# Two-layer gated cross-attention and routed experts on one core: counts read per expert, a second row buffer, and an earlier weight conversion

## The reference, cut to what matters

```python
# layer 0: 8 experts, the best 4 for each token, hidden size 1024
routing_weights = softmax(x @ router_w)
topk_weights, topk_indices = top_k(routing_weights, 4)
topk_weights = topk_weights / sum(topk_weights)
h = gelu(einsum('bsd,edh->bseh', x, up_w))
out = sum over the chosen e of topk_weight * (h_e @ down_w[e])
# layer 1: 8 experts, the best 2, biases b1 and b2, exact gelu
x = x + tanh(g_ffn[layer]) * out
```

## Time and profile before

| | us |
|---|---|
| median of 3 runs | 1605.39 (1602.2 to 1613.03) |
| the profiled execution | 1604.2 |
| its span, first to last instruction | 1602.3 |
| experts of layer 0 in it, from the first branch | 500 to 962 |
| experts of layer 1 in it, lists and end included | 1289 to 1602.3 |

### The profile page before, as it was taken

The page is one execution under the profiler, slowest core; times in us unless marked ns, Lnnn a source line. Parts: engine busy times, 40 slices in busy tenths (PEclk is TensorE's granted clock), DMA queues, the critical chain, the costliest instruction groups (busy, mean ns, idle before and its releaser), DMA issues. The chain is left out here.

```text
span 1602.3 us, 25436 instructions
## 1 busy us (share of the span) xinstructions
PE 1392.9 (87%) x9908; PEld 1288.8 (80%) x9908; DVE 834.8 (52%) x1654; ACT 713.1 (45%) x1375; POOL 552.5 (34%) x389
## 2 busy tenths in 40 slices
PE   5899989899867999999989995999889678987996
PEld 5776858768647899899889995988888668987996
DVE  3655656655664446446435223556666865455421
ACT  3354444444343454444444443454343425443553
POOL 1200001001025466566565441122120266566543
PEclk8899999999987999999999997998989769998998
DMA  3302031110115343443442223021202165444222
GB/s 128 120 24 67 27 95 43 52 61 27 66 51 156 94 86 81 116 106 92 105 104 47 47 42 100 24 88 41 72 30 80 54 193 119 102 106 109 48 42 35
DMA packets 72147, 123.30 MB, mean 77 GB/s; under 512 B 7440, under 2 KB 53152, under 8 KB 71968
## 3 DMA queue, kind: packets, MB, share of 16 engines
q1 hardware_dynamic: 46816, 81.92, 15.6%
q0 software_dynamic: 25152, 39.01, 13.4%
HBM read 96.12 MB, written 24.79 MB: 75 GB/s over the span
## 5 line engine op out<-in xcount | busy, mean ns | idle before, releaser
L2324 DVE TENSOR_TENSOR m_hidden_lo<-m_act_out,m_hidden_hi 128x512 fp32r<-128x512 f32 x224 | 162.6, 727 | 393.9 <-ACT m_hidden_hi L2267 368.5
L395 PE MATMUL banks<-m_down_hi,m_hidden_hi 128*128 128x256 f32 x896 | 267.9, 299 | 17.5 <-DVE m_hidden_lo L2324 11.3
L395 PE MATMUL banks<-m_down_hi,m_hidden_lo 128*128 128x256 f32 x896 | 263.7, 294 | 1.5 <-issue 1.5
L395 PE MATMUL banks<-m_down_lo,m_hidden_hi 128*128 128x256 f32 x896 | 263.9, 295 | 0.3 <-issue 0.3
L395 PEld LDWEIGHTS banks<-m_down_hi,m_hidden_hi 128*128 128x128 f32 x896 | 181.6, 203 | 22.2 <-issue 20.4
L395 PE MATMUL banks<-m_xt_hi,m_up_hi 128*128 128x256 f32 x640 | 186.6, 291 | 6.4 <-issue 6.4
L395 PE MATMUL banks<-m_xt_lo,m_up_hi 128*128 128x256 f32 x640 | 183.2, 286 | 0.0
L395 PE MATMUL banks<-m_xt_hi,m_up_lo 128*128 128x256 f32 x640 | 183.1, 286 | 0.0
L395 PEld LDWEIGHTS banks<-m_down_hi,m_hidden_lo 128*128 128x128 f32 x896 | 181.1, 202 | 1.7 <-issue 1.7
L395 PEld LDWEIGHTS banks<-m_down_lo,m_hidden_hi 128*128 128x128 f32 x896 | 181.5, 203 | 0.6 <-issue 0.6
L2401 POOL DMA_INDIRECT m_other_block<-rows,list_i x116 | 120.8, 1042 | 148.5 <-DVE list_i L1453 100.6
(11 more groups left out here) (367 smaller groups left out, 3555.0 us busy)
## 6 DMA issues: line engine op xcount, KB each, us to landing
stage<-in_down SPq DMA_DIRECT2D x22, 512.0 KB
stage<-in_ctx_cols SPq DMA_DIRECT2D x26, 402.0 KB
stage<-in_ctx_rows SPq DMA_DIRECT2D x20, 512.0 KB
stage<-in_up SPq DMA_DIRECT2D x20, 512.0 KB
m_stage<-in_up SPq DMA_DIRECT2D x11, 512.0 KB
m_stage<-in_down SPq DMA_DIRECT2D x10, 512.0 KB
rows<-xn SPq DMA_DIRECT2D x8, 528.0 KB, 3.7
stage<-in_ctx_picked SPq DMA_DIRECT2D x8, 512.0 KB
```

The costliest lines, as they stand in the source:

```text
L395: mm = q.e.matmul(dst, a, b, start=first and n == 0, stop=last and n == 2, skip_group_check=True)
L2324: q.e.tensor_tensor(lo, m.act[(n * HP + h) % ACTS], f32(hi), ALU.subtract).then_inc(*hidden_lo.mark((layer, n, h)))
```

## The change

Three things change.

1. Each engine loads the count of an expert when it reaches that expert's branches, after block (e, 0), instead of all eight at the head (`count_of`, called by `blocks`). The counting matmul and the copy of its result come ahead of the four steps that write the lists.
2. Blocks with j > 1 have two row buffers, by j even or odd. The second lies in the memory of the tables `onehot`, which are not needed while experts are computed. Block (e, j) gathers (e, j+3) now, and block (e, 0) gathers both (e, 2) and (e, 3), at its head. POOL's block (e, 0) is a function of its own, `gpsimd_opening`.
3. DVE converts quarters 2 and 3 in one go ahead of the low part of pair 0.

```diff
@@ counts
-        def counts(q, layer):
+        def count_of(q, layer, e):
+
             q.wait_ge(*route_dve.of("count", layer))
-            return [q.e.snap(q.e.value_load(counts_i[0:1, e:e + 1], min_val=0, max_val=BATCH * TOK)) for e in range(E)]
+            return q.e.snap(q.e.value_load(counts_i[0:1, e:e + 1], min_val=0, max_val=BATCH * TOK))
...
-        def blocks(q, layer, held, own, e, j, block):
+        def blocks(q, layer, own, e, block):
+            further(q, layer, count_of(q, layer, e), own, e, 1, block)
+
+        def further(q, layer, held, own, e, j, block):
...
@@ row buffers
-                m.other = sb(n + "other_block", [P, BT, ROW], F32, st)[:, :, :]
+                m.other = [sb(n + "other_block", [P, BT, ROW], F32, st)[:, :, :], rows_there]
...
-            return m.other if j > 1 or (e, j) == (0, 0) else m.second if j else m.first
+            return m.other[j % 2] if j > 1 or (e, j) == (0, 0) else m.second if j else m.first
...
-            return numbered(e, j - 1) if j > 2 else numbered(e - 1, NB - 1) if j == 2 else numbered(e - 1, j)
+            return numbered(e, j - 2) if j > 3 else numbered(e - 1, NB - 4 + j) if j > 1 else numbered(e - 1, j)
@@ vector_block
+            if more:
+                q.wait_ge(*down_done.of(layer, n - 1, HP - 1))
+                convert(q, "d", [quarter(layer, e + 1, x) for x in range(KD, 4)])
             for h in range(HP):
                 vector_low(q, layer, e, j, h)
...
-                if more and h >= 2:
-                    q.wait_ge(*down_done.of(layer, n - 1, HP - 1))
-                    convert(q, "d", [quarter(layer, e + 1, KD + h - 2)])
@@ gpsimd_gather
-            if j == 2 and (layer or e):
-
-                q.e.wait_ge(other_in.sem, q.e.snap(others_begun[0]))
+            if j in (2, 3) and (layer or e):
+
+                q.e.wait_ge(there.sem, q.e.snap(others_begun[j % 2]))
@@ gpsimd_block
-            n, more = numbered(e, j), j == 0 and e + 1 < E
-            gpsimd_added(q, layer, n - 2)
-            if 0 < j < NB - 1:
-                gpsimd_there(q, layer, e, j + 1)
-            if (e, j) == (1, 0):
+            n = numbered(e, j)
+            if j != 1:
+                gpsimd_added(q, layer, n - 2)
+            if j == 0:
+                gpsimd_opening(q, layer, e)
+                return
+            if 1 < j < NB - 2:
+                gpsimd_there(q, layer, e, j + 2)
+            gpsimd_add(q, layer, e, j)
+            if j + 3 < NB:
+                gpsimd_gather(q, layer, e, j + 3)
+
+        def gpsimd_opening(q, layer, e):
+
+            n, following = numbered(e, 0), [quarter(layer, e + 1, x) for x in range(4)] if e + 1 < E else []
+            gpsimd_gather(q, layer, e, 2)
+            gpsimd_gather(q, layer, e, 3)
+            if e == 1:
                 gpsimd_gather(q, layer, 2, 0)
-            if more:
-                convert(q, "p", [quarter(layer, e + 1, x) for x in range(KD)])
+            convert(q, "p", following[0:KD])
             if n:
-                gpsimd_add(q, layer, e, j)
-            if j + 2 < NB:
-                gpsimd_gather(q, layer, e, j + 2)
-            if more:
-                convert(q, "p", [quarter(layer, e + 1, x) for x in range(KD, 4)])
+                gpsimd_add(q, layer, e, 0)
+            gpsimd_there(q, layer, e, 2)
+            gpsimd_there(q, layer, e, 3)
+            convert(q, "p", following[KD:4])
+            if following:
                 gpsimd_gather(q, layer, e + 1, 1)
-                if e and e + 2 < E:
-                    gpsimd_gather(q, layer, e + 2, 0)
-            if j == 0:
-                convert(q, "p", ahead(layer, e - 1))
+            gpsimd_added(q, layer, n - 1)
+            if e and e + 2 < E:
+                gpsimd_gather(q, layer, e + 2, 0)
+            convert(q, "p", ahead(layer, e - 1))
```

More of the change, by code:

```diff
@@ L1517, in tensor_count, with vector_count, vector_finish_lists @@
                 *route_pe.mark(use))
-        def vector_finish_lists(q, layer):
+        def vector_count(q, layer):
             use = ("count", layer)
             q.wait_ge(*route_pe.of(*use))
+            q.wait_ge(*added.of(layer - 1, "all"))
+            q.e.tensor_copy(counts_i[:, :], gen.of(use)[0:1, 0:E]).then_inc(*route_dve.mark(use))
+        def vector_finish_lists(q, layer):
             q.wait_ge(*route_dve.last())
-            q.e.tensor_copy(counts_i[:, :], gen.of(use)[0:1, 0:E]).then_inc(*route_dve.mark(use))
             spare = col("spare").unsqueeze(1).to_broadcast([P, E * NB - 1, BT])
@@ L2130, in blocks @@
             before_, passed = [s.count for s in own], dict(q.passed)
-            with q.e.If(held[e] > BLOCK * j):
+            with q.e.If(held > BLOCK * j):
                 block(q, layer, e, j)
-                blocks(q, layer, held, own, e, j + 1, block)
+                further(q, layer, held, own, e, j + 1, block)
             with q.e.Else():
@@ L2149, in tensor_down @@
             if n == 0:
-                q.wait_ge(*route_dve.of("count", layer))
+                q.wait_ge(*route_dve.of("put", layer, BATCH - 1, TT - 1))
             if layer and f == 0:
@@ L2223, in tensor_experts @@
                     tensor_block(q, layer, e, 0)
-                blocks(q, layer, held, own, e, 1, tensor_block)
+                blocks(q, layer, own, e, tensor_block)
             for f in range(HT):
@@ L2292, in scalar_experts @@
                     scalar_block(q, layer, e, 0)
-                blocks(q, layer, held, own, e, 1, scalar_block)
+                blocks(q, layer, own, e, scalar_block)
             scalar_y(q, layer, E * NB - 1, exp[layer].w_last[(E - 1) % 2])
@@ L2364, in vector_experts @@
             vector_place(q, layer, b)
+            vector_count(q, layer)
             vector_mark(q, layer, b, 0)
@@ L2476, in gpsimd_experts @@
             gpsimd_gather(q, layer, 1, 0)
-            held = counts(q, layer)
             for e in range(E):
                 gpsimd_block(q, layer, e, 0)
-                blocks(q, layer, held, own, e, 1, gpsimd_block)
+                blocks(q, layer, own, e, gpsimd_block)
             gpsimd_added(q, layer, E * NB - 2)
-            q.e.wait_ge(other_in.sem, q.e.snap(others_begun[0]))
-            q.e.nop().then_inc(*rested.mark())
+            for there, begun in zip(other_in, others_begun):
+                q.e.wait_ge(there.sem, q.e.snap(begun))
+                q.e.nop().then_inc(*rested.mark())
             gpsimd_add(q, layer, E, 0)
@@ L2569, in _ @@
         def _(e):
-            others_begun[:] = [e.alloc_register("others_begun")]
+            others_begun[:] = [e.alloc_register(f"others_begun{i}") for i in range(2)]
             adds_begun[:] = [e.alloc_register("adds_begun")]
```

25 lines of the change are left out of this document (12 added, 13 removed).

## The result

The changed kernel takes 1641.08 us (median of 4 runs, 1633.33 to 1644.4), the kernel before 1605.64 beside it: a ratio of 1.0208, 95% interval 1.0157 to 1.0259. It is slower: the interval leaves 1 clearly out, though not a difference of less than 2%. The forecast was 1624 in a range of 1592 to 1645: the direction and the place were right, the size of the pauses was too small, and the result lies near the upper end of the range. The profiled execution took 1642.2 us, 38.0 more than that of before, where the sum had +19.

A forecast was written before the change was run, and what follows sets the result against it. PE was taken to bound the expert stages. Terms -1 - 10.5 + 25 + 7 + 1 - 2.5 = +19 on the profile's 1604.2 gave 1623.2, 1624 against the median; own range 1610 to 1645, over all rivals down to 1592.

The forecast's parts named there:

- Part 1, counts: At both expert heads: PE gains from fewer loads, ACT's m_y starts later behind POOL's mark; -1 us, between -8.6 and +5.
- Part 2, L2410: Layer 0: PE's four pauses for POOL's word that rows are there go, 8.1 us plus clock; -10.5 us.
- I let nothing take their place: Assumed ACT's wait for POOL's mark would not replace PE's four removed pauses, so all 10.5 us are gained.
- The pauses: Layer 0, experts 1 to 5: PE waits for pair 0 behind late-fetched quarters; +25 us idle (13 to 32), +7 clock.
- PE reaches it 2 us later: Expert 1 of layer 0: PE's later arrival set against two more gathers of 1.32 us; its pause taken as 4 us.
- its 6 us: Casts slowing POOL's gathers, 1.3 us in each of five experts, some 6 us in all; left out of the sum.
- Layer 1: Conversions ahead of pair 0 cost +1 us (0 to 6), counted with layer 0's experts 0, 6, 7; -2.5 behind expert 5.
- -2.5 behind expert 5: Layer 1: the late conversion leaves the last pair's way and a count load comes; -2.5 us, between 0 and -3.5.
- A: Rival: quarters 2 and 3 reach DVE before PE finishes the ups, so the five pauses don't arise; 1591 us, chance 0.18.
- B: Rival: the five pauses are short, 13 us, with little clock loss (+2); 1606 us, no measurable difference, chance 0.2.
- C: Rival: ACT's wait for POOL's mark replaces PE's at j = 3; 5 of 10.5 us stay away, 1629 us; inside forecast's 0.62.

The follow-up runs named there:

- e7: e1 with POOL's word that the adds have landed put ahead of the gathers at each head of the experts; 1595.42 us, 0.9959 of the kernel before.
- e1: Changed kernel with part 3 undone: down quarters 2 and 3 converted after pairs 2 and 3 again; 1599.44 us, 0.9977 of the kernel before.
- e11: Kernel before with part 2 alone: second row buffer and POOL's new order; 1599.57 us, 0.9977 of the kernel before.
- e10: e6 with the low part of quarter 2 of layer 1 made by DVE instead of POOL; 1597.66 us, 0.9975 of the kernel before.
- e3: Kernel before with part 3 alone: down quarters converted ahead of pair 0; 1601.07 us, 0.9998 of the kernel before.
- e5: Changed kernel with SP fetching quarters 2 and 3 before the next attention's two pieces, which DVE converts after its pairs; 1605.77 us, 1.0030 of the kernel before.
- e2: Changed kernel with POOL's low part of quarter 0 ahead of the gathers (e, 2) and (e, 3); 1618.97 us, 1.0097 of the kernel before.
- e4: Kernel before with part 1 alone: counts loaded at each expert; 1600.57 us, 0.9981 of the kernel before.
- e6: Changed kernel with part 3 in layer 1 only; 1603.57 us, 1.0011 of the kernel before.
- e9: e7 with the gather of (2, 0) ahead of the other two in expert 1; 1592.13 us, 0.9934 of the kernel before.
- e12: e9 plus the edits of e10; 1594.09 us, 0.9942 of the kernel before.

## Why the prediction was right, and where it was too small

- **Part 1, counts: right in kind.** Forecast -1 for the heads, and that ACT would wait for POOL's word behind the gathers (0, 2) and (0, 3): m_y was released by exactly that, and PE's 3.28 became 3.06. It began at 506.6, 5.4 us later than before, where the working had 0.2 to 2.2: the four gathers went at 498.26 and not at 494.9, behind those of (0, 1) and (1, 0). Alone the part gave nothing measurable; e7's trace shows that the gain at the head of layer 0 was there to be had and sat behind these gathers.
- **Part 2, L2410: -10.5 forecast, -12.1 in the trace.** The step "I let nothing take their place" was wrong for a kernel without the pauses (e1, e11): there ACT's wait takes about half of the idle time. In the changed kernel the term held; there ACT's waits for POOL's word are gone but one.
- **The pauses: the mis-sized term.** Forecast 25 idle and 7 of clock, measured 34.6 and 10.7: 13.3 of the 19 us by which the sum was short. In expert 2 the working gave 4.6 us, of which the sum took 4, and the trace 6.90. Counted from DVE's last low part of the old expert: the four gathers and the start behind them took 6.4 us instead of 5.3 (1.29, 1.83, 1.43 and 0.95), so the low part of quarter 0 and SP's fetch came 1.2 later than forecast. Landing, both casts and the low part then went nearly as worked out, and pair 0 was ready 20.2 us behind that point against 19.3. PE came to it at 13.4, not 14.7: it had run at full clock behind the change of expert, which the forecast allowed for in expert 4 only. Expert 1 was furthest off, 7.83 against 4. It has six gathers ahead of its low part, and they took from 551.50 to 560.96, 9.5 us for 8 in the working. "PE reaches it 2 us later" came true (15.4 us behind DVE's last low part, against 13.4 in expert 2). But two gathers more (2.6) less these 2 us make expert 1's pause longer than expert 2's, and the sum gave both 4.
 The Trainium skill, "SBUF — State Buffer", section "Who interferes with whom", has the rule that a DVE cast in a two-port mode can starve descriptor generation; the prediction left its 6 us out of the sum. The trace agrees that gathers are slower beside DVE: those beside its casts and low parts (625.1 to 629.7) took 1.29, 1.83 and 1.43 us, the one behind them 0.95. It doesn't show that casts alone do it. The third gather met only a subtraction (628.70 to 629.70).
- **Layer 1: right in sum by luck, wrong in its parts.** Forecast +1 for the rest and -2.5 behind expert 5; measured -2.7 for all, but before's two waits of 4.87 and 4.83, which no other kernel has, are 4.9 us of that; against e1 the changed kernel loses 5.5 there. PE's wait behind expert 5 stayed at 6.0. The -2.5 was taken for certain once the cast left the last pair's way; but the same cast, moved ahead, lets POOL's low part run beside the pairs, which then costs 3.2 us on the way of the last pair. e10 gives the 2.5 back, and in e3, with part 3 alone, 1.6 of it came.
 The same section of the Trainium skill says that a copy can enter a two-port mode and then fully blocks against GpSimd. The rows agree: 3.34 us for 128x2 words beside POOL, 0.16 without. A low part of a pair, 3.81 us for 0.69, is the case of two SBUF inputs that the prediction quotes.
- **Rivals.** A and B fell: DVE found no data before 638.2, while PE had come at 636.9 and each pause was over 5 us. C was right as a mechanism and near its size, but in e1 and e11 and not in the changed kernel.
- **Not in the forecast:** 3.5 us before the experts and 3.2 in the second attention. The second is a difference that kernels with and without the change show (above). Up to the lists of layer 0 the fourteen traces have 487.5 to 494.7 us (before 487.5, now 491.0), without an order by the parts of the change. So no run shows these 6.7 of the 38.0 us to be an effect of the change; the medians differ by 35.4.

## What to carry to other kernels

When work is moved ahead of something that is waited for, its inputs must be early too: follow the moved step back to its fetch, and that to the instruction that frees its slot. Two parts of a change that are each free alone (0.998 and 1.000 here) can cost 2% together, so the changed order has to be traced as a whole; an earlier place in SP's order took most of it back. When two traces are compared, begin and end the stretches at the same instruction, and look in a third trace whether a difference belongs to the kernel or to one execution. And a low part on POOL should not lie beside DVE's short steps that PE waits for.

## What the runs showed of the hardware

- A DVE copy of 128x2 words took 3.34 to 3.40 us at the places shown (the changed kernel, e5) where it met POOL's subtraction of 128x1024 words, and 0.16 without it (e10). Over the fourteen traces 55 such copies overlapped a subtraction of POOL's, and 45 of them took 2.0 to 3.4 us; none of the other 2521 took over 1. The record of the changed kernel's begins 0.4 us before POOL's and ends with it (1503.57 to 1506.91, against 1503.95 to 1506.87). What such a step loses follows what it meets, not its own length: 3.2 us for the copy, 3.1 for a low part of 0.69, 2.1 for one of 1.23.
- Indirect gathers of 0.95 us took up to 2.04 us on POOL beside DVE's work (e2, the first behind its low part). Over the fourteen traces the 868 with no DVE instruction beside them took at most 1.02; of the 1259 that met subtractions alone a tenth took 1.43 or more, the longest 1.78.
- The two adds at the start of expert 1 of layer 1 landed 3.6 to 3.8 us after their issue where SP fetched nothing beside them (e3, e4), 4.1 to 5.9 beside two quarters (e1, e6, e9, e11) and 7.6 to 8.8 beside four (e10, e12).
- "issue" as the releaser of PE's five longest waits was DVE's low part, which ended 0.1 us before PE began.
